# State space layer: the output product from rounded parts on TensorE

## The reference, cut to what matters

```python
zxbcdt = u @ W_in                       # u: 256 x 512, W_in: 512 x 2320
conv = silu(causal convolution of 4 taps over xBC)
y, _ = ssd(x * dt, A * dt, B, C, 64)    # 16 heads of 64
y = y + x * D
y = y * silu(z)
var = mean(y ** 2, axis=-1)
y = y * rsqrt(var + 1e-5) * norm_scale
return y @ W_out                        # 256 x 1024 times 1024 x 512
```

## Time and profile before

| | |
|---|---|
| median of three runs | 1031.43 us |
| the profiled execution's own time | 1029.74 us |
| its span | 1028.0 us |
| mean granted TensorE clock (share of 2.4 GHz) | 0.992 |
| TensorE matmul busy | 985.4 us (96%) |
| VectorE busy | 737.4 us (72%) |
| ScalarE busy | 572.3 us (56%) |
| GpSimd busy | 290.8 us (28%) |
| DMA read and written | 103.24 and 4.91 MB |

### The profile page before, as it was taken

How to read it: one execution, slowest core, us unless ns; L and a number is a source line. 1 busy time by engine, 2 the same in 40 slices (tenths; PEclk the granted TensorE clock), 3 DMA queues, 4 the chain that set the end, 5 groups by cost and what they waited for, 6 DMA issues and landing times.

```text
span 1028.0 us, 17980 instructions
## 1 busy us (share of the span) xinstructions
PE 985.4 (96%) x6609; PEld 788.0 (77%) x6609; DVE 737.4 (72%) x1456; ACT 572.3 (56%) x1250; POOL 290.8 (28%) x210
## 2 busy tenths in 40 slices
PE   7999999999999699999999999999999999989996
PEld 5545689999998567678888888888888887968653
DVE  3566536555552679979888898989978787658566
ACT  3435354444441421088777768677687777836634
POOL 6910044444442400000002132422405423113412
PEclk9999999999999999999999999999999999999999
DMA  8560066666650433122013453424313203065100
GB/s 274 134 248 1 1 186 227 217 213 220 224 186 1 143 93 97 52 86 59 2 43 80 63 121 75 78 74 83 96 38 87 84 1 99 2 244 230 67 1 20
DMA packets 65980, 109.15 MB, mean 106 GB/s; under 512 B 19409, under 2 KB 44145, under 8 KB 64754
## 3 DMA queue, kind: packets, MB, share of 16 engines
q1 hardware_dynamic: 65906, 108.17, 35.0%
HBM read 103.24 MB, written 4.91 MB: 105 GB/s over the span
## 4 chain that ended last, share of the span: by engine, by line
PE 76%; DVE 14%; ACT 7%; issue 2%; DMA 1%; POOL 1%; SPq 0%; DVEq 0%; ACTq 0%; POOLq 0%
PE PS L1695 14%; PE PS L1568 13%; PE PS L1684 10%; PE PS L1672 8%; PE PS L1587 6%; PE PS L1657 4%; PE PS L1787 3%; PE PS L1709 2%; DVE scores L1182 2%; ACT scores L844 2%; DVE pL L1243 2%; PE PS L1468 1%; PE PS L1830 1%; PE PS L1627 1%; PE PS L1431 1%
## 5 line engine op out<-in xcount | busy, mean ns | idle before, releaser
L1243 DVE TENSOR_TENSOR pL<-PS,pH 128x512 fp32r<-128x512 f32 x256 | 175.8, 687 | 49.5 <-ACT pH L871 47.2
L871 ACT ACTIVATE pH<-PS 128x512 fp32r<-128x512 f32 x249 | 147.6, 596 | 98.7 <-PE PS L1684 97.9
L844 ACT ACTIVATE scores<-scores,nmX 128x512 f32<-128x512 f32 x256 | 184.9, 723 | 12.8 <-DVE nmX L1186 12.8
L1182 DVE TENSOR_SCALAR_CACHE_REDUCE scores<-PS 128x512 f32<-128x512 f32 x256 | 172.6, 682 | 13.4 <-PE PS L1672 13.0
L1695 PE MATMUL PS<-pH,kvH 128*128 128x256 f32 x512 | 164.5, 321 | 0.0
L1684 PE MATMUL PS<-ident,scores 128*128 128x128 f32 x1024 | 157.5, 276 | 3.7 <-DVE pL L1243 1.6
L1684 PEld LDWEIGHTS PS<-ident,scores 128*128 128x128 f32 x1024 | 117.1, 140 | 36.0 <-issue 18.0
L1695 PE MATMUL PS<-pL,kvH 128*128 128x256 f32 x512 | 143.9, 281 | 0.0
L1695 PE MATMUL PS<-pH,kvL 128*128 128x256 f32 x512 | 143.7, 281 | 0.0
L1695 PEld LDWEIGHTS PS<-pH,kvH 128*128 128x128 f32 x512 | 96.7, 189 | 2.8 <-issue 1.8
L1695 PEld LDWEIGHTS PS<-pL,kvH 128*128 128x128 f32 x512 | 97.2, 190 | 0.0
(11 more groups left out here) (311 smaller groups left out, 2224.6 us busy)
## 6 DMA issues: line engine op xcount, KB each, us to landing
rawG<-in_wg SPq DMA_DIRECT2D x16, 768.0 KB, 5.7
rawU<-in_wu SPq DMA_DIRECT2D x16, 768.0 KB, 7.2
rawD<-in_wd SPq DMA_DIRECT2D x16, 768.0 KB, 6.2
wrow<-in_w SPq DMA_DIRECT2D x11, 512.0 KB, 5.2
xn<-in_w1t SPq DMA_DIRECT2D x11, 512.0 KB
wturned<-turned SPq DMA_DIRECT2D x4, 1056.0 KB, 14.3
wb<-w_rows SPq DMA_DIRECT2D x32, 128.0 KB, 3.3
wqX<-in_wqX SPq DMA_DIRECT2D x16, 256.0 KB, 2.6
```

The lines of the kernel that those rows point to most:

```text
L844: act.activation(at, at, ACT.Exp, bias=nmX[:, p % 2, h, q:q + 1], accum_out=csum[:, p % 2, NT * h + q, c:c + 1]).then_inc(exp_done, 1)
L871: act.activation(pH[:, i % 4], PS[:, 2 + i % 2, :].rearrange("p (k t) -> p k t", t=T), ACT.Copy).then_inc(pH_ready, 1)
L1182: dve.tensor_scalar(sp_[:, h, q, c * CH:(c + 1) * CH], PS[:, 4 * q + h, :], 1.0, None, ALU.mult, ALU.max, accum_out=cmax[:, h, q, c:c + 1] ...
L1243: dve.tensor_tensor(pL[:, i % 4], PS[:, 2 + i % 2, :].rearrange("p (k t) -> p k t", t=T), pH[:, i % 4].bitcast(F32), ALU.subtract).then_in ...
```

## The change

1. `project` takes three float32r products for each row tile instead of one float32 product: high part of yn with high part of W_out, low part of yn with high part, high part of yn with low part.
2. ScalarE writes `ynH` (float32r) where it wrote `yn`. VectorE adds `ynL` = yz times norm scale minus ynH, one instruction of 128x256 for each m, placed behind `yz` and ahead of `masked(m+2)`. It waits for ScalarE's ynH of the same m. TensorE's wait ahead of `project` is for ynL instead of yn.
3. GpSimd rounds W_out to `woutH0` (m 0 to 3) and `woutH1` (m 4 to 7), one copy of 128x2048 each: the first behind its first four `weighted`, the second behind `cv4` and ahead of the other four. `woutH1` lies on the memory of `xp`, `woutH0` on new memory.
4. VectorE makes `woutL` = W_out minus high part, in place, two instructions of 128x2048 behind the last tap and ahead of `xdt`, each behind GpSimd's copy of its half.
5. Ahead of the narrow product, `stay_awake(1)` follows the first group of transposes and `stay_awake(3)` the second.

```diff
+        early = ExitStack()
+        woutL = sb("woutL", [P, IT, D], F32R, early)
+        early.close()
         wout = A("wout", [P, IT, D])
...
+        early = ExitStack()
+        woutH1 = sb("woutH1", [P, IT // 2, D], F32R, early)
+        early.close()
         xp = A("xp", [P, CT, CONV - 1 + T]); cv = A("cv", [P, CT, T]); act_ = A("act_", [P, CT, T])
...
-        yn = A("yn", [P, 2, T]); y2 = A("y2", [P, 2, T]); y2s = A("y2s", [P, T])
+        woutH0 = A("woutH0", [P, IT // 2, D], F32R); ynH, ynL = (A(n, [P, 2, T], F32R) for n in ("ynH", "ynL")); y2 = A("y2", [P, 2, T]); y2s = A("y2s", [P, T])
...
+            def high_out(half, room):
+                pool.tensor_copy(room[:], wout[:, half * IT // 2:(half + 1) * IT // 2]).then_inc(ssm_consts, 1)
+
             for m in range(IT // 2):
                 weighted(m)
+            pool.wait_ge(wout_in, 16)
+            high_out(0, woutH0)
             pool.wait_ge(ssm_dve.sem, ssm_dve.at("cv4", 2))
+            high_out(1, woutH1)
             for m in range(IT // 2, IT):
                 weighted(m)
...
-                    act.activation(yn[:, m % 2], yz[:, m % 2], ACT.Copy, scale=ns[:, m:m + 1]).then_inc(yn_ready, 1)
+                    act.activation(ynH[:, m % 2], yz[:, m % 2], ACT.Copy, scale=ns[:, m:m + 1]).then_inc(yn_ready, 1)
...
+            for half, room in enumerate((woutH0, woutH1)):
+                part = slice(half * IT // 2, (half + 1) * IT // 2)
+                dve.wait_ge(ssm_consts, 6 + half)
+                dve.tensor_tensor(woutL[:, part], wout[:, part], room[:].bitcast(F32), ALU.subtract).then_inc(ssm_dve.sem, 1)
...
                 dve.tensor_tensor(yz[:, m % 2], yt[:, m % 2], zs[:, m], ALU.mult).then_inc(yz_ready, 1)
+                dve.wait_ge(yn_ready, m + 1)
+                wait(dve, o_done, m - 1)
+                dve.scalar_tensor_tensor(ynL[:, m % 2], yz[:, m % 2], ns[:, m:m + 1], ynH[:, m % 2].bitcast(F32), ALU.mult, ALU.subtract).then_inc(ssm_dve.sem, 1)
...
                 turn_tile(4, t, 4)
+                stay_awake(1 + 2 * t, 7)
...
-                return pe.matmul(PS[:, t, :], yn[:, m % 2, t * P:(t + 1) * P], wout[:, m, :], start=(m == 0), stop=(m == IT - 1))
+                high = woutH0[:, m] if m < IT // 2 else woutH1[:, m - IT // 2]
+                for c, (v, w) in enumerate(((ynH, high), (ynL, high), (ynH, woutL[:, m]))):
+                    mm = pe.matmul(PS[:, t, :], v[:, m % 2, t * P:(t + 1) * P], w, start=(m == 0 and c == 0), stop=(m == IT - 1 and c == 2))
+                return mm
...
-            pe.wait_ge(wout_in, 16)
...
-                    pe.wait_ge(yn_ready, m)
+                    pe.wait_ge(ssm_dve.sem, ssm_dve.at("ynL", m))
...
-            pe.wait_ge(yn_ready, IT)
+            pe.wait_ge(ssm_dve.sem, ssm_dve.at("ynL", IT))
```

More of the change, by code:

```diff
@@ L290, in perceiver @@
         ssm_act = Marks(sem("ssm_act"), dte=2, tap0=2, tap1=2, silu0=2, tap2=2, silu1=2, tap3=2, silu2=2, tap4=2, silu3=2, silu4=2)
-        ssm_dve = Marks(sem("ssm_dve"), dta=1, a=1, cv0=2, cv1=2, cv2=2, gm=1, cv3=2, cv4=2, xdt=NT)
+        ssm_dve = Marks(sem("ssm_dve"), dta=1, a=1, cv0=2, cv1=2, cv2=2, gm=1, cv3=2, cv4=2, woutL=2, xdt=NT, ynL=IT)
         late_pe = Marks(sem("late_pe"), ss=1, yo=NT, xqT0=1, gu0=2, xqT1=1, gu1=6, hqT0=2, hqT1=3)
```

## The result

Over 20 runs of each the changed kernel took 1033.72 us in the median (1028.08 to 1037.98) and the kernel before 1031.61 (1027.94 to 1035.80). The ratio is 1.0026, 95% interval 1.0014 to 1.0039: 2.7 us slower (1.4 to 4.0); the two medians lie 2.1 apart. The forecast was 1.6 us slower, 1033.0.

A forecast was written before the change was run, and what follows sets the result against it. TensorE's 3.64 us a turn bounds the output loop, a second cycle of 3.38 close beside it. Late start +3.3, fillers -1.5 and loop -0.2 sum to +1.6: 1031.43 becomes 1033.0 us, range 1030.4 to 1035.6.

The forecast's parts named there:

- woutL and high_out behind the taps, +3.3: Between last tap and xdt: VectorE's subtractions and GpSimd's second copy run serially, starting the output loop 3.3 us later.
- the rule named in the prediction: VectorE and GpSimd at SBUF: whichever starts first holds the port pair for a whole instruction; copy serial too, +3.3 us.
- VectorE and GpSimd overlap: Rival for the work before xdt: copies leave VectorE alone, start only +0.6 to +1.4 us, total 1030.7 us; chance 0.16.
- Fillers, -1.5: Ahead of the narrow product: fillers keep TensorE at 2.4 GHz into the wide product, saving 1.5 us, bounds 0 and 1.8.
- clock not kept: Rival at the wide product: four fillers are too few to keep the clock, total 1034.5 us; chance 0.30.
- The loop, -0.2: Output loop and tail: 0.4 us gained, 0.2 lost to memory meetings; net -0.2, bounds -0.5 to +0.4.
- the ring: Output loop's cycle masked, yt, yz, yn, y2, exp, next masked: 3.38 us, claimed to set the period after the change.
- the steady meeting of ynL with the sum of y2: In the loop, VectorE's ynL and GpSimd's sum share the way to memory: cost taken as 0.2 us, possible 0 to 0.75.
- weighted(4) comes some 4 us later: nothing: GpSimd's weighted(4), delayed some 4 us, is used two turns into the output loop, so it costs nothing.
- TensorE's turn, 3.13: In the output loop, TensorE's turn falls from 3.64 to 1.40 + 0.93 + 0.80 = 3.13 us, 0.51 less.
- TensorE's results stay over 1 us ahead of their users: In the output loop, TensorE finishes over 1 us before its results are needed, so the 3.38 us cycle sets the period.
- The clock falls in the new wait: Rival at the output loop's start: TensorE's clock drops while waiting for xdt, +1.2 to +1.7 us, total 1034.4; chance 0.14.

The follow-up runs named there:

- e12: Changed kernel with GpSimd's weighted(4) and (5) issued after masked(1), (6) and (7) behind the first two sums of y2: ratio to the kernel before 1.0022.
- e1: Kernel before with only the four fillers ahead of the narrow product added: ss at 68.63 us against 69.65, ratio 0.9999.
- e3: Changed kernel without VectorE's two subtractions, the third product taking W_out's high part again (output lacks the low parts): ss at 68.64 us, ratio to before 0.9986.
- e4: Changed kernel with ten more fillers in TensorE's wait for xdt, behind log_decay(0): ss at 72.10 us against 72.06, ratio to the kernel before 1.0012.
- e7: Changed kernel with e5 and e6 together and VectorE's first subtraction moved ahead of the last taps: ss at 68.47 us, ratio to the kernel before 0.9961.
- e5: Changed kernel with ScalarE's exp for m+2 moved ahead of y2(m): ss at 72.04 us against 72.06, ratio to the kernel before 0.9999.
- e6: Changed kernel with W_out's high parts copied earlier, by ScalarE instead of GpSimd: ss at 71.60 us against 72.06, ratio to the kernel before 1.0002.
- e8: e1, with the old float32 product, and ScalarE's exp for m+2 moved ahead of y2(m): ss at 68.63 us, ratio to the kernel before 0.9954.

## Why the prediction was right, and where it was not

*woutL and high_out behind the taps, +3.3: right in mechanism and nearly in size.* From the last tap to the start of xdt I had 7.2 us; it was 7.1. A subtraction takes 2.29 alone (2.27 forecast), the copy 1.90 (its rows give 1.95 where the prediction has 1.8 to 1.9), the turn of `weighted` 0.84 (0.8; e12 has woutL(1) without it). The one thing that no row had shown, a one-input copy against VectorE, is shown by woutL(0): 4.01 for 2.29. By the rule named in the prediction (the Trainium skill, SBUF — State Buffer, "SBUF: two separate sides") this trace agrees: the copy, which started first, keeps its full length and the subtraction stands still (4.01). Against e1 the term is 3.02 us, against e3 3.03. The rival "VectorE and GpSimd overlap" is dead.

*Fillers, -1.5: the clock was kept, the size was 1.02.* TensorE won 1.7 us on the 64 records (15.75 to 14.06), and then 0.39 went to the wait for `silu0` and more behind it: `silu0`, made from VectorE's first taps behind the softplus, came no sooner at all (17.82 us behind the first transposes for 17.83), where I had allowed 0.4, and the product of B and C began 1.14 earlier, not 1.5. The last tap passes on 1.03. The rival "clock not kept" is out.

*The loop, -0.2: wrong sign; it was +0.41, just outside my bounds of -0.5 to +0.4.* This is the step that failed. I let the whole loop run at the ring's period from the start. The period was right: 3.38 to 3.39 in the changed kernel from masked(3) on. It is that of the earlier trace rows, so the steady meeting of ynL with the sum of y2, for which I took 0.2, cost nothing. But masked(2) came 6.10 us behind masked(0) (5.53 before) and masked(3) 9.74 (8.92 before). VectorE's first turn meets GpSimd's `weighted`, which high_out(1) and the subtractions have pushed later. The first two masked, before and after:

```profile
963.02 2.77 DVE L1322 TENSOR_TENSOR mh<-decay,gm 128x768 f32<-128x768 f32 x2 [0.31 <-ACT decay L923]
...
968.82 1.52 DVE L1338 TENSOR_TENSOR mh<-decay,gm 128x768 f32<-128x768 f32 x1
970.77 1.28 DVE L1338 TENSOR_TENSOR mh<-decay,gm 128x768 f32<-128x768 f32 x1 [0.43 <-ACT decay L935]
```

Masked(1) ends 3.23 us behind the start of masked(0), for 2.77 before. The wait of 0.43 for `decay` is not the cause: in e4, where `decay` came sooner, masked(1) began at 1.45, took 1.79 and ended at 3.24. Another 0.10 at masked(2) is the low clock, under which log_decay(2) comes late; e4 has masked(2) that much sooner, and loses it again beside `weighted`. Further on GpSimd has

```profile
972.92 1.22 POOL L667 TENSOR_TENSOR ua<-upto,avH 128x512 fp32r<-128x512 f32 x1
974.10 1.22 POOL L667 TENSOR_TENSOR ua<-upto,avL 128x512 fp32r<-128x512 f32 x1
975.27 1.12 POOL L685 COPY y2s<-y 128x256 f32<-128x256 f32 x1
```

and, on VectorE in the same execution, a masked that was 0.96 long before:

```profile
974.92 1.21 DVE L1338 TENSOR_TENSOR mh<-decay,gm 128x768 f32<-128x768 f32 x1 [0.51 <-ACT decay L935]
```

In all 0.82 is lost by masked(3), of which the shorter period won back 0.44 by masked(7) (23.28 against 22.90). I had counted "weighted(4) comes some 4 us later: nothing", looking only at TensorE, its reader, and not at VectorE, which stands beside it. In e3, with less delay, the loss is 0.42 at masked(2) and the gain just pays for it. The tail was 5.40 (5.37 before), where I had 5.4.

*TensorE's turn, 3.13:* it was 3.33 (e7), 0.10 more for the products and 0.10 more for log_decay. In the changed kernel the ring of 3.38 hid the error; it decided e5 and e7, which were to bring more than came: e5 1.0 to 1.5 us, and e7's ss came 0.5 to 1.2 later than expected. Nor do TensorE's results stay over 1 us ahead of their users: my own rows give log_decay 0.7 ahead of exp (5.25 and 5.94 behind masked), and in the changed kernel it is 0.2 to 0.3.

*The clock falls in the new wait:* it fell, as that rival said, but its price of 1.2 to 1.7 us was not paid (e4). TensorE at 1.2 GHz had room beside VectorE and ScalarE, which paced those turns. The room is small: in e5 and e6, where the low stretch reached 0.7 and 1.0 us further into the loop, ScalarE waited for TensorE.

The sum by the layer: +3.02 - 1.02 + 0.41 = +2.41, for +1.6 forecast. 0.5 of the 0.8 between them is the fillers' size, 0.6 the loop, less 0.3 of the start. So the direction and the large term were understood; that the total came so near is in part luck, since the start's 0.3 was taken off the other two.

The experiments point to e7 as the best of the changed line: 1.18 us below the kernel before in the layer, 0.9961 (0.9945 to 0.9978) in whole runs. But e1 alone gives 1.02 of it, and e7's gain over e1 is 0.16 us. From masked(3) to masked(7) e7 wins 0.67 on e1 (13.31 for 13.98), but it comes to masked(3) 0.46 later (9.38 for 8.92): its first two masked take 3.48 beside GpSimd, 2.77 in e1. So not everything around the product is hidden in e7.

## What to carry to other kernels

Before making the busiest engine faster, measure the ring beside it: here TensorE led by 0.26 us a turn, and the 0.31 a turn saved on it could bring no more. Preparations on VectorE and GpSimd that both read SBUF have to be added up one behind the other, and what they push later has to be followed to whoever works beside it, not only to whoever reads it. Four cheap fillers at the right wait were worth more than the new product (1.02 us and 0.16).

## What the runs showed of the hardware that I had not expected

- A GpSimd copy with one input and a VectorE subtraction with two go one behind the other. A lead of 0.03 us was enough for the copy to keep its length: 1.90 and 4.01 us in the changed kernel. The other order, VectorE first by so little, is in no run.
- A low clock on an engine that doesn't pace can cost nothing or a few tenths: nothing that shows in the changed kernel, where it ended 5.5 us behind masked(0), and 0.31 us, by its trace, in e6, where it ended at 6.5.
- The moment at which the layer begins varied from 918.79 (e12) to 926.34 (e1) in profiles of kernels whose instructions ahead of it are the same. Stretches at 1.2 GHz ahead of it differ too (7 us of them in e7, 17 in the changed kernel), though they don't explain all of it: e12, e7 and e8 have 7 us each and begin at 918.79, 920.21 and 922.10. So two profiles' spans can't be compared to a few us, while times inside a layer repeat to 0.03.
- e1 and e8 have the same layer time to 0.01 us, yet ratios of 0.9999 and 0.9954, whose intervals do not meet. The granted clock of the whole runs goes with it: its mean is 0.992 over e1's runs and 0.991 over the 35 of the kernel before beside them, but 0.994 over e8's and 0.990 over the 35 beside those. In those runs of the kernel before, 0.001 more clock goes with about 0.9 us less, so that by this estimate 3.7 of the 4.0 us between the means of e8 and its before are the clock. Why e8's runs had more of it stays open; I take no verdict of 0.2 to 0.4% from the whole runs of e1 to e12 alone.
